# Attention scores in groups of three tiles instead of two, in two halves of six PSUM banks

## What is computed

```python
def sdpa(qh, kh):                      # layer 0: two maps of 16 heads, head size 4
    scores = jnp.einsum('bhqd,bhkd->bhqk', qh, kh) * scale
    a = jax.nn.softmax(scores, axis=-1)
    return jnp.einsum('bhqk,bhkd->bhqd', a, v)
...
o = attn1 - lam * attn2
...
attn = jax.nn.softmax(jnp.einsum('bhqd,bhkd->bhqk', q, k) * scale, axis=-1)   # layer 1: 16 heads, size 8
out = jnp.einsum('bhqk,bhkd->bhqd', attn, v)
```

## Time and profile before

| | |
|---|---|
| median of 3 runs | 846.43 us (844.07 to 846.95) |
| the profiled execution, its own time | 843.49 us |
| its span in the profile | 841.7 us |
| PE busy | 773.7 us (92%) |
| ACT busy | 763.4 us (91%) |
| DVE busy | 543.6 us (65%) |
| POOL busy | 36.2 us (4%) |
| products with the values, `ps_pv` (L904), on PE | 410.0 us |
| exponentials (L732), 768 | 725.9 us |
| granted TensorE clock, mean | 0.993 |

### The profile page before, as it was taken

How to read it: one execution, slowest core, us unless ns; L and a number is a source line. 1 busy time by engine, 2 the same in 40 slices (tenths; PEclk the granted TensorE clock), 3 DMA queues, 4 the chain that set the end, 5 groups by cost and what they waited for, 6 DMA issues and landing times.

```text
span 841.7 us, 17809 instructions
## 1 busy us (share of the span) xinstructions
PE 773.7 (92%) x6751; PEld 269.5 (32%) x6751; DVE 543.6 (65%) x1200; ACT 763.4 (91%) x856; POOL 36.2 (4%) x56
## 2 busy tenths in 40 slices
PE   8888889999999899998999999998998899999997
PEld 6122223332433233332332223332242333423332
DVE  7877884867674686656685666747768376377322
ACT  3979989989899998999989999999988899899985
POOL 4100000000000100001000010000000000000000
PEclk9999999999999999999999999999999999999998
DMA  3827347602538025650357315390254603302500
GB/s 104 179 44 147 94 99 181 90 1 77 138 94 115 14 77 138 136 73 14 125 134 123 42 52 146 81 150 8 94 133 112 96 2 124 78 2 78 137 13 14
DMA packets 42452, 74.88 MB, mean 89 GB/s; under 512 B 6552, under 2 KB 8216, under 8 KB 42360
## 3 DMA queue, kind: packets, MB, share of 16 engines
q1 hardware_dynamic: 40560, 68.12, 37.5%
q0 software_dynamic: 1744, 5.44, 2.1%
q10 hardware_dynamic: 56, 0.10, 0.0%
HBM read 36.84 MB, written 35.65 MB: 86 GB/s over the span
## 4 chain that ended last, share of the span: by engine, by line
PE 54%; ACT 25%; DVE 10%; issue 8%; DMA 2%; SPq 1%; DVEq 0%; ACTq 0%
ACT probs L732 25%; PE ps_pv L904 20%; PE ps_s L885 14%; PE ps_misc L753 7%; PE ps_misc L757 6%; PE ps_misc L758 4%; PE ps_misc L746 2%; DMA q_ab<-shifts 1%; DMA parts_dram<-qk_parts 1%; DVE pv_sb L1389 1%; ACT ff_out L687 0%; DVE qk_parts L1191 0%; DVE qk_parts L1193 0%; SPq L469 0%; DVE h_lo L1143 0%
## 5 line engine op out<-in xcount | busy, mean ns | idle before, releaser
L732 ACT ACTIVATE probs<-ps_s 128x1024 f32<-128x1024 f32 x768 | 725.9, 1046 | 42.7 <-PE ps_s L885 41.2
L904 PE MATMUL ps_pv<-probs,v_aug 128*32 128x512 f32 x3072 | 410.0, 606 | 9.9 <-DVE pv_sb L1389 4.4
L885 PE MATMUL ps_s<-q_ab,k_ab 18*128 18x512 f32 x1024 | 130.2, 497 | 25.7 <-ACT probs L732 22.2
L885 PEld LDWEIGHTS ps_s<-q_ab,k_ab 18*128 18x128 f32 x1024 | 49.4, 182 | 186.0 <-ACT probs L732 151.9
L904 PEld LDWEIGHTS ps_pv<-probs,v_aug 128*32 128x32 f32 x3072 | 61.6, 108 | 105.8 <-issue 73.1
L1141 DVE CAST h_hi<-ff_out 128x512 fp32r<-128x512 f32 x64 | 27.3, 427 | 101.0 <-ACT ff_out L685 99.6
L757 PE MATMUL ps_misc<-h_hi,k_w 128*128 128x512 f32 x192 | 86.3, 449 | 0.3
L885 PE MATMUL ps_s<-q_c,k_c 32*128 32x512 f32 x512 | 64.8, 495 | 21.1 <-ACT probs L732 20.9
L1389 DVE STREAM_TRANSPOSE pv_sb<-ps_pv 128x512 f32<-128x512 f32 x48 | 34.4, 716 | 74.5 <-PE ps_pv L904 73.0
L758 PE MATMUL ps_misc<-h_lo,k_w 128*128 128x512 f32 x192 | 76.5, 398 | 0.0
L757 PEld LDWEIGHTS ps_misc<-h_hi,k_w 128*128 128x128 f32 x192 | 36.1, 188 | 87.0 <-issue 52.8
(11 more groups left out here) (167 smaller groups left out, 558.5 us busy)
## 6 DMA issues: line engine op xcount, KB each, us to landing
parts_dram<-qk_parts SPq DMA_DIRECT2D x94, 256.0 KB, 3.7
parts_dram<-qk_parts SPq DMA_DIRECT2D x16, 512.0 KB, 2.8
q_c<-parts_dram SPq DMA_DIRECT2D x32, 256.0 KB, 4.9
k_c<-parts_dram SPq DMA_DIRECT2D x32, 256.0 KB, 7.2
q_ab<-parts_dram SPq DMA_DIRECT2D x60, 128.0 KB, 4.8
k_ab<-parts_dram SPq DMA_DIRECT2D x60, 128.0 KB, 6.0
x_ring<-in_L_attn_x_dram POOLq DMA_DIRECT2D x7, 256.0 KB, 3.0
out_dram<-x_ring POOLq DMA_DIRECT2D x7, 256.0 KB, 2.9
```

The source lines that it names most:

```text
L732: nc.scalar.activation(probs[:, U.slot(s), 2 * half:2 * half + 2], ps_s[:, 2 * pair:2 * pair + 2], ACT.Exp, bias=-SCALE[1] * BOUND[1] if U ...
L885: ins = nc.tensor.matmul(ps_s[:, bank, :], k[row:row + n, slot, c * P:(c + 1) * P], q[row:row + n, slot, :], start=True, stop=True)
L904: ins = nc.tensor.matmul(ps_pv[32 * j:32 * j + 32, :], v_aug[:, U.v, c, a:a + 32], probs[:, U.slot(s), j, :], start=c == 0 and not odd, st ...
```

## The change

Tiles are numbered through the whole program. Group t (class `Triple`) holds the tiles 3t to 3t+2 and writes three of the six banks, the lower half for even t and the upper for odd. There are 512 groups where there were 768 pairs and 384 steps. One exponential takes a group (1536 columns); where the three tiles belong to two layers (10 groups), it is cut into one of 512 and one of 1024 columns, since scale and bias differ. `probs` holds the same 12 tiles, now as one ring. A group waits until the exponential of group t-2 has ended.

Four tiles a step and three a group make four groups in three steps. Ahead of the values of step S, PE makes groups up to `ahead(S)`, the fewest groups that hold all tiles of the steps up to S-1 and two tiles of S. In steps with S % 3 == 1, called the middle steps below, a further group stands between the values and the jobs (`ahead_of_jobs`), on PE and on ACT alike. The table of jobs is not touched.

```diff
+class Triple:
+    def __init__(self, t):
+        self.t = t
+        self.banks = 3 * (t % 2)
+        self.probs = 3 * t % PROBS
+        self.tiles = [Tile(3 * t + i) for i in range(3)]
...
+def ahead(S):
+    return min(triples_for(4 * S + 2), TRIPLES)
...
+def ahead_of_jobs(u, s):
+    S = STEPS * u + s
+    return min(ahead(S) + (S % 3 == 1 and not exact_first(u, s)), TRIPLES)
...
+            def exp(tr):
+                wait(act, pv_made, (3 * tr.t + 2 - PROBS) // 4 + 1)
+                act.wait_ge(scores_made, tr.t + 1)
+                for a, b, layer in tr.runs():
+                    ins = nc.scalar.activation(probs[:, tr.probs + a:tr.probs + b], ps_s[:, tr.banks + a:tr.banks + b], ACT.Exp,
...
-                    for half in range(2):
-                        pair = U.pairs(s)[half]
-                        wait(act, pv_made, S - 2)
-                        act.wait_ge(scores_made, 2 * S + half + 1)
+                    for t in range(done, ahead_of_jobs(u, s)):
+                        exp(Triple(t))
...
+            def scores(tr):
+                for tile in tr.tiles:
+                    operands_there(tile)
+                wait(pe, exps_made, tr.t - 1)
+                for i, tile in enumerate(tr.tiles):
...
+                    ins = nc.tensor.matmul(ps_s[:, tr.banks + i, :], k[row:row + n, slot, c * P:(c + 1) * P], q[row:row + n, slot, :],
                                            start=True, stop=True)
-                    if j % 2 == 1:
-                        ins.then_inc(scores_made, 1)
+                ins.then_inc(scores_made, 1)
...
-                pe.wait_ge(exps_made, 2 * S + 2)
+                pe.wait_ge(exps_made, triples_for(4 * S + 4))
...
-                    scores(U, s)
+                    for t in range(done, ahead(S)):
+                        scores(Triple(t))
...
                     if s >= 2:
                         pv(U, s - 2)
                     elif u > 0:
                         pv(Unit(u - 1), STEPS - 2 + s)
+                    for t in range(done, ahead_of_jobs(u, s)):
+                        scores(Triple(t))
                     run(items, holds)
```

More of the change, by code:

```diff
@@ L23 @@
 RING = 4
+PROBS = 12
 DQK = (4, 8)
@@ L206, in __init__, with runs, triples_for, exact_first @@
         self.times = self.b // 2 if self.layer == 1 else self.b
[L208 to L212, removed]
+class Triple:
[4 more added lines that the diff above has]
+        self.tiles = [Tile(3 * t + i) for i in range(3)]
+    def runs(self):
+        layers = [tile.U.layer for tile in self.tiles]
+        cut = next((i for i in range(1, 3) if layers[i] != layers[0]), 3)
+        return [(a, b, layers[a]) for a, b in ((0, cut), (cut, 3)) if a < b]
+class Tile:
+    def __init__(self, n):
+        S, self.j = n // 4, n % 4
+        self.U, self.s = Unit(S // STEPS), S % STEPS
+def triples_for(tiles):
+    return -(-tiles // 3)
+def ahead(S):
+    return min(triples_for(4 * S + 2), TRIPLES)
+def exact_first(u, s):
+    items = TABLE[u].get(s, [])
+    return bool(items) and items[0][0] in ("exact0", "exact1")
+def ahead_of_jobs(u, s):
+    S = STEPS * u + s
+    return min(ahead(S) + (S % 3 == 1 and not exact_first(u, s)), TRIPLES)
 def values_free(layer, b):
@@ L247, in two_layers @@
         k_c = sb("k_c", [P, 8, N], F32R)
-        probs = sb("probs", [P, 3, 4, N], F32)
+        probs = sb("probs", [P, PROBS, N], F32)
         v_aug = sb("v_aug", [P, 2, T, VROW], F32)
@@ L722, in _ @@
                 nc.scalar.copy(qk_parts[:, i, 0, :], bank_of((name, 0))).then_inc(first_hi, 1)
+            done = 0
             for u in range(UNITS):
[L725 removed]
                 for s in range(STEPS):
[L727 to L733 removed]
+                    for t in range(done, ahead_of_jobs(u, s)):
+                        exp(Triple(t))
+                    done = ahead_of_jobs(u, s)
                     if (u, s) == (1, 0):
@@ L738, in _ @@
                         job(item)
+            for t in range(done, TRIPLES):
+                exp(Triple(t))
             for item in EPILOGUE:
@@ L872, in exact_max, with operands_there @@
                     pe.sem_inc(gen_made[layer], GEN_MADE[layer])
[L874 to L885, removed]
+            def operands_there(tile):
+                U, s = tile.U, tile.s
+                if tile.j != 0:
+                    return
+                if U.u == 0:
+                    if s == 0:
+                        warm(WARM_AGAIN)
+                        wait_taken(pe, ("fast", 0, "k", 0))
+                        pe.wait_ge(shift_loaded["A"], SHIFTED)
+                    elif s == 4:
+                        wait_taken(pe, ("fast", 0, "k", 1))
+                    elif s == 8:
+                        pe.wait_ge(qk_loaded["A"], loaded(U))
+                        pe.wait_ge(first_k_loaded, 16 * TILES)
+                        pe.wait_ge(k_ones_loaded, K_ONES)
+                elif s == 0:
+                    pe.wait_ge(qk_loaded[U.stack], loaded(U))
+                    if U.layer == 0:
+                        pe.wait_ge(shift_loaded[U.stack], SHIFTED * (U.times + 1))
@@ new lines, in scores @@
+            def scores(tr):
[3 more added lines that the diff above has]
+                for i, tile in enumerate(tr.tiles):
+                    U, j = tile.U, tile.j
+                    g, c = tile.s // 4, tile.s % 4
+                    q, k, slot0, _ = operands(U)
+                    n = ROWS[U.layer] + (PARTS if U.layer == 0 else 0)
+                    row, slot = TILE_ROWS * j, slot0 + g
+                    ins = nc.tensor.matmul(ps_s[:, tr.banks + i, :], k[row:row + n, slot, c * P:(c + 1) * P], q[row:row + n, slot, :],
@@ L903, in pv @@
                     a = (4 * g + j) * VHEAD + (0 if odd else VW)
-                    ins = nc.tensor.matmul(ps_pv[32 * j:32 * j + 32, :], v_aug[:, U.v, c, a:a + 32], probs[:, U.slot(s), j, :],
+                    ins = nc.tensor.matmul(ps_pv[32 * j:32 * j + 32, :], v_aug[:, U.v, c, a:a + 32], probs[:, (4 * S + j) % PROBS, :],
                                            start=c == 0 and not odd, stop=c == 3 and odd == 1)
@@ L929, in _ @@
                 for s in range(STEPS):
[L930 to L945, removed]
-                    scores(U, s)
+                    S = STEPS * u + s
+                    for t in range(done, ahead(S)):
+                        scores(Triple(t))
+                    done = ahead(S)
                     items = TABLE[u].get(s, [])
-                    exact = items and items[0][0] in ("exact0", "exact1")
-                    holds = heads_within(int(items[0][0][-1]), items[0][1]) if exact else None
+                    holds = heads_within(int(items[0][0][-1]), items[0][1]) if exact_first(u, s) else None
                     if s >= 2:
@@ L953, in _ @@
                         pv(Unit(u - 1), STEPS - 2 + s)
+                    for t in range(done, ahead_of_jobs(u, s)):
+                        scores(Triple(t))
+                    done = max(done, ahead_of_jobs(u, s))
                     run(items, holds)
+            for t in range(done, TRIPLES):
+                scores(Triple(t))
             for s in range(STEPS - 2, STEPS):
```

8 lines of the change are left out of this document (6 added, 2 removed).

## The result

The changed kernel takes 863.25 us (median of 4 runs, 860.79 to 866.49) where the kernel before took 846.69 in the same comparison: a ratio of 1.0205, with a 95% interval of 1.0165 to 1.0244. It is slower by 17 us. The forecast was 865, 19 us above the 846.4 of the kernel before. The profiled execution took 863.47 us, with a span of 861.7.

What follows compares the result with a forecast made beforehand. PE and ACT bound the kernel in turns; the change makes PE the bound almost everywhere. Seven loop-like stretches at + 3.0 us, less 2 elsewhere, lift the profiled 843.5 to 862.5; 2.9 to the median gives 865 us, range 838 to 882.

Steps and rivals of the forecast that it cites:

- What a group of three costs: Score matmuls on PE: a group of three costs the same 0.44 us as one of four; bounds 0.33 and 0.44.
- PE, part by part: PE's scores: 128 more groups at 0.44 us each, 56 us in all; PE busy near 825 us.
- The loop: 48 steps from 99.89 to 102.9 us, 3.0 more per loop, with PE the bound almost everywhere.
- The hand-over of 2.11 us: Last group of three steps waits for the exponential of the middle step's first group: 0.60 + 1.46 + 0.05 us.
- the loop's run of three steps with no job: One run in the loop goes at ACT's 5.37 us instead of PE's 4.76, + 0.6 us.
- collisions: Loop time above the larger of PE's and ACT's needs: 2.9 us before, 0.8 added after.
- From the loop to the program: Whole program: 7 loop-like stretches at + 3.0 give + 21 us, the start and other job-poor parts - 2, so + 19.
- the last 2.9 us: Step from profiled execution to median of the runs, which lies 2.9 us above it: 862.5 becomes 865.
- ACT's part: ACT's exponentials: 246 fewer instructions at 0.06 us save 15 us of work; bounds 0 and 42.
- Groups cost by the tile: Rival, scores on PE: a group of three takes 0.33 us, so the kernel gets faster, 827 us; chance 0.14.
- The fourth group hides in PE's waits: Rival: the 56 us added fit into PE's 68 us idle, no change, 846 us; chance 0.08.
- Late ReLUs: Rival, middle steps: ACT takes jobs up to 1.34 us later, slower still, 883 us; chance 0.10.

Runs made afterwards that it cites:

- e1: Changed kernel, but from the third group on each group makes only two of its three score tiles, still 512 groups: 861.86 us, 1.0219.
- e7: Kernel before, with one of the four score tiles of a step left out: 841.68 us, 0.9964.
- e4: Changed kernel with the fourth group moved from between values and jobs to the front of the next step, two groups in a row: 864.97 us, 1.0277.
- e3: Changed kernel with every exponential cut into one of 1024 and one of 512 columns, 502 more ACT instructions: 870.55 us, 1.0322.
- e5: Kernel before, with PE making the scores of middle steps three times, reported to ACT only after the third: 889.39 us, 1.0522.
- e6: Changed kernel, ACT's program alone moved: in middle steps it takes the job ahead of the fourth group's exponential: 870.93 us, 1.0313.

## Why the prediction was right

- **What a group of three costs.** 0.44 us was right, and e1 and e7 show that width does not matter from two tiles to four. The pack rule that I quoted from the Trainium skill ("TensorE: Matmul & The Clock Gate", "Measured speedup vs the span model") holds here as far as a whole run can tell: a group of two, three or four tiles takes 0.43 to 0.44 us.
- **PE, part by part.** I forecast about 825 us of busy time and 260 for scores; it is 823.4 and 262.6. The 49.7 us of rise stay a little under the 56 that the sum counted; where the rest went is not shown.
- **The loop.** 102.9 forecast, 102.76 measured, each stretch within 0.1 us. The hand-over of 2.11 us from a group to the one two behind it is in e4's rows exactly. One term was wrong inside a right sum: the loop's run of three steps with no job was put at ACT's 5.37 us; it takes 4.97 us (5.50 before), four groups at PE's own pace and one short wait. PE's timeline in unit C after, at both ends of this run and between:

```profile
388.99 0.50 PE L954 MATMUL ps_s<-q_c,k_c 32*128 32x512 f32 x3
...
390.42 0.50 PE L954 MATMUL ps_s<-q_c,k_c 32*128 32x512 f32 x3
...
391.84 0.50 PE L954 MATMUL ps_s<-q_c,k_c 32*128 32x512 f32 x3
392.53 0.50 PE L954 MATMUL ps_s<-q_c,k_c 32*128 32x512 f32 x3 [0.19 <-ACT probs L721]
...
393.96 0.50 PE L954 MATMUL ps_s<-q_c,k_c 32*128 32x512 f32 x3
```

  The wait makes the hand-over again (392.53 - 390.42 = 2.11), so this run goes at what PE and the hand-over need, 4.76 + 0.23 = 4.99. The 5.37 is there where bare steps follow each other for longer, in the first unit (34.42 - 29.05):

```profile
29.05 0.50 PE L954 MATMUL ps_s<-q_ab,k_ab 18*128 18x512 f32 x3 [0.58 <-ACT probs L721]
...
34.42 0.50 PE L954 MATMUL ps_s<-q_ab,k_ab 18*128 18x512 f32 x3 [0.58 <-ACT probs L721]
```

  So the loop's sum was 0.4 us too high in this term. Without that it comes to 101.7, which leaves 1.1 us for collisions, and the 0.8 for them was a guess. That the loop came out within 0.14 us is in part luck. (The 5.37 itself is a small slip: 0.918 + 0.431 is 1.35 and not 1.34, and four of them are 5.40.)
- **From the loop to the program.** Here two misses cancelled. The start of the values of a step in PE's timeline, first before and then after, for the steps 48, 80 and 272 of the program (of 384; the four loops run from 80 to 272):

```profile
123.50 1.07 PE L904 MATMUL ps_pv<-probs,v_aug 128*32 128x512 f32 x8
126.61 1.06 PE L972 MATMUL ps_pv<-probs,v_aug 128*32 128x512 f32 x8 [0.25 <-issue]
...
193.77 1.07 PE L904 MATMUL ps_pv<-probs,v_aug 128*32 128x512 f32 x8 [0.44 <-ACT probs L732]
197.95 1.07 PE L972 MATMUL ps_pv<-probs,v_aug 128*32 128x512 f32 x8 [0.36 <-issue]
...
593.38 1.06 PE L904 MATMUL ps_pv<-probs,v_aug 128*32 128x512 f32 x8 [0.51 <-ACT probs L732]
608.96 1.06 PE L972 MATMUL ps_pv<-probs,v_aug 128*32 128x512 f32 x8 [0.70 <-ACT probs L721]
```

  The kernel after is 3.1, 4.2 and 15.6 us behind at these steps, and 20.0 at the end of the span. The four loops add 11.4 us where the forecast has 12.0. The first 48 steps add 3.1 us where the sum had most of its gain of 2 us, and the last 112 steps add 4.4, where 3.0 for each 48 steps would be 7.0. Why the first units lose is not shown. The rise of 20.0 us against 19 forecast is right in the loops by its mechanism and right in the whole by luck. The same holds for the last 2.9 us, the distance of the median from the profiled execution: it is 3.2 us before (846.69 - 843.49) and - 0.2 after (863.25 - 863.47).
- **ACT's part.** The fixed cost of an instruction was put at 0.06 us; it is 0.04 to 0.05. Two exponentials of 1024 columns in the row of fourteen of the earlier trace rows, the third and the ninth:

```profile
479.73 1.95 ACT L732 ACTIVATE probs<-ps_s 128x1024 f32<-128x1024 f32 x2
...
485.14 2.03 ACT L732 ACTIVATE probs<-ps_s 128x1024 f32<-128x1024 f32 x2
```

  Their pace is (485.14 - 479.73) / 6 = 0.902, and that of 1536 columns is 1.331 (the rows at e3). With the same cost per column in both, the fixed part is 3 x 0.902 - 2 x 1.331 = 0.044, with 0.01 of doubt. So 246 fewer instructions give about 11 us, not 15. The Trainium skill ("ScalarE: Activation LUTs", "What ACT_TABLE_LOAD costs") gives an overlap of 93 ns, from which the prediction had 23 us; the rows here show 0.13 and 0.12 us (1.03 - 0.90 and 1.45 - 1.33). The pace of 0.918 in the prediction had one pause in it. I also expected near 700 us busy for the exponentials; it is 722.8. The median of one is 1.45 us as forecast, but where PE sets the pace they follow each other later and overlap less, and each shows more of its 1.45. ACT's busy time did not fall (761.9 against 763.4), so the saving was not visible there; e3 shows it by putting it back.
- **The rivals.** "Groups cost by the tile" fell with e1 and e7. "The fourth group hides in PE's waits" fell with the result, and e5 shows why it had to: in the pair form, 45 of 56 us show up although 43.2 us of waits stood there. "Late ReLUs" had 883 us and fell with the result; e6, which takes them early, is slower still.
- **Where my own account was short.** I treated PE's idle time as cover that the new work uses up, and only counted 2.9 us of collisions in a loop. That understated the cost in the pair form (e5: 868 to 876 expected, 889 measured). It did no harm to the forecast, as I read it, because the change lengthens the slack of the hand-over at the same time as it adds the work. The prediction had the two in one sum, without seeing how large each may be alone: 45 us in e5, in the form of before and ahead of the report to ACT, 17 to 20 in the change. That the slack makes this difference is argued, as said at e3.

## What to carry to other kernels

When four small matmuls run side by side on the array, count the groups and not the matmuls: the same tiles in four groups of three cost a third more TensorE time than in three groups of four (175.4 us against 130.2 here), as long as other work stands between the groups. Idle time of an engine that sits in a loop of two engines is slack only as far as the other engine has work in hand; take it from the hand-over (end to start, start to ready, the other's pace) and not from the sum of waits. And saving instructions on the second-busiest engine is worth little when it puts work onto the busiest.

## What the runs showed of the hardware

- A row-tiled wave, the group of this document, costs 0.44 us behind work of another shape and 0.22 behind another such wave (e4: 0.66 for two; e5: 0.90 for three).
- An activation's cost beyond its columns is 0.04 to 0.05 us when another follows at once (paces of 0.902 us for 1024 columns and 1.331 for 1536), though one alone lasts 0.17 us longer than its columns (1.032 less 0.862, as the prediction works out).
- The duration of one score matmul says nothing of a group's cost: it reads 0.49 to 0.50 us with two (e1), three (e7, the kernel after) or four side by side. The start of the next kind of work shows the cost.
